# Attention values with v stationary in four column tiles, softmax sums from ScalarE's accumulator, own heads picked by DMA, and the end of the layer in later slots

## The reference, cut to what matters

```python
xn = _layernorm(x)
x = x + mamba(xn) + experts(xn)       # layer 0: conv, selective scan over N = 16 states; top-1 of 8 experts
xn = _layernorm(x)
x = x + attn(xn) + ffn(xn)            # layer 1

def attn(x, Wq, bq, Wk, bk, Wv, bv, Wo, bo):      # 16 heads of 8 channels, window of 64
    q, k, v = (_split_heads(x @ W + b) for W, b in ((Wq, bq), (Wk, bk), (Wv, bv)))
    scores = einsum('bhqd,bhkd->bhqk', q, k) / sqrt(8) + _sliding_window_mask(s, 64)
    probs = softmax(scores)
    return merge_heads(einsum('bhqk,bhkd->bhqd', probs, v)) @ Wo + bo

def ffn(x, w_gate, w_up, w_down):                 # int weights times 1/127, 384 hidden
    return (silu(x @ wg.T) * (x @ wu.T)) @ wd.T
```

## Time and profile before

| | before |
|---|---|
| time, median of 3 runs | 1190.73 us (1190.70 to 1194.21) |
| the profiled execution: its own time | 1193.12 us |
| its span in the trace | 1191.1 us, 13478 instructions |
| PE / DVE / ACT / POOL busy, share of the span | 78% / 71% / 51% / 35% |
| mean granted clock of PE | 0.923 of 2.4 GHz |

### The profile page before, as it was taken

One profiled execution on the slowest core, in us unless ns is written; L12 is line 12 of the kernel. 1 busy time (PEld: TensorE's weight loads), 2 busy tenths in 40 slices (PEclk: granted clock), 3 DMA queues, 4 the chain that ended last, 5 costly groups with the idle time before them and its releaser, 6 DMA issues.

```text
span 1191.1 us, 13478 instructions
## 1 busy us (share of the span) xinstructions
PE 923.4 (78%) x4474; PEld 585.3 (49%) x4474; DVE 849.0 (71%) x1301; ACT 613.0 (51%) x1410; POOL 411.1 (35%) x234
## 2 busy tenths in 40 slices
PE   3553888857887788778887788878787878788786
PEld 2412676734554455545454455545554545445555
DVE  7772543669779877888688868886978788767232
ACT  2142555635655655564566455655645564654542
POOL 2274222233622362237213722363226423532000
PEclk9566999987999899999999899989998999999998
DMA  8163878843322332233223321333233223430000
GB/s 277 40 216 125 235 234 294 239 110 86 81 65 75 90 82 73 66 79 89 73 70 90 89 73 54 90 92 87 54 80 87 76 66 83 99 80 1 10 1 9
DMA packets 79540, 116.65 MB, mean 98 GB/s; under 512 B 4848, under 2 KB 40048, under 8 KB 79344
## 3 DMA queue, kind: packets, MB, share of 16 engines
q1 hardware_dynamic: 73184, 108.99, 33.5%
q0 software_dynamic: 6288, 6.82, 2.5%
HBM read 103.73 MB, written 12.06 MB: 97 GB/s over the span
## 4 chain that ended last, share of the span: by engine, by line
PE 37%; DVE 19%; issue 17%; POOL 13%; ACT 10%; DMA 3%; SPq 0%; POOLq 0%; DVEq 0%; ACTq 0%
PE y_bank L1151 11%; DVE hst L705 7%; POOL hc L1066 7%; PE more L1240 7%; POOL xs_d L1034 3%; POOL x_res L1050 3%; ACT pexp L983 3%; PE work_l L1232 3%; DVE dBu L697 2%; ACT pT L988 2%; PE work_l L1226 2%; PE work L1232 2%; PE work L1170 2%; DMA hst<-in_hidden 1%; PE more L1248 1%
## 5 line engine op out<-in xcount | busy, mean ns | idle before, releaser
L1066 POOL TENSOR_TENSOR hc<-hst,bcr 128x1024 f32<-128x1024 f32 x116 | 280.2, 2415 | 607.8 <-DVE dBu L697 607.8
L1151 PE MATMUL y_bank<-hc,pk 128*128 128x512 f32 x512 | 275.0, 664 | 68.6 <-POOL hc L1066 59.7
L705 DVE TENSOR_TENSOR_SCAN hst<-dA,dBu 128x1024 f32<-128x1024 f32 x128 | 291.6, 2278 | 5.7 <-ACT dA L901 4.9
L1151 PEld LDWEIGHTS y_bank<-hc,pk 128*128 128x128 f32 x512 | 100.6, 208 | 183.9 <-POOL hc L1066 83.9
L901 ACT ACTIVATE dA<-dt,neg_a 128x511 f32<-128x511 f32 x256 | 171.4, 726 | 17.3 <-DVE hst L705 15.8
L697 DVE TENSOR_TENSOR dBu<-dtu,bcr 128x1024 f32<-128x1024 f32 x128 | 157.9, 1234 | 12.7
L1240 PE MATMUL more<-vw,pT 96*128 96x99 f32 x1024 | 131.0, 280 | 37.3 <-ACT pT L988 25.9
L1240 PEld LDWEIGHTS more<-vw,pT 96*128 96x128 f32 x1024 | 121.2, 194 | 69.3 <-issue 38.1
L988 ACT COPY pT<-work 96x512 f32<-96x512 f32 x64 | 37.2, 581 | 157.4 <-PE work L1232 157.4
L820 DVE TENSOR_REDUCE nmax<-work 128x4 f32<-128x384 f32 x64 | 35.4, 554 | 62.6 <-PE work L1226 62.6
L988 ACT COPY pT<-work_l 96x512 f32<-96x512 f32 x64 | 37.2, 581 | 63.9 <-PE work_l L1232 63.9
(11 more groups left out here) (296 smaller groups left out, 1422.0 us busy)
## 6 DMA issues: line engine op xcount, KB each, us to landing
bcr<-bc_d SPq DMA_DIRECT2D x128, 512.0 KB, 4.9
qbd<-in_wx SPq DMA_DIRECT2D x8, 578.0 KB, 3.9
attn<-in_wx SPq DMA_DIRECT2D x8, 578.0 KB, 4.3
pT<-in_wx SPq DMA_DIRECT2D x8, 578.0 KB, 5.7
kT<-in_wx SPq DMA_DIRECT2D x8, 578.0 KB, 5.3
vw<-in_wx SPq DMA_DIRECT2D x8, 578.0 KB, 5.0
xs_d<-rbuf POOLq DMA_DIRECT2D x1, 2560.0 KB, 9.7
hst<-in_hidden SPq DMA_DIRECT2D x8, 256.0 KB, 5.8
```

The source lines that it names most:

```text
L705: v.tensor_tensor_scan(hst[n % 2][:].rearrange("p h t -> p (h t)"), dA[n % 2][:].rearrange("p h t -> p (h t)"), dBu[:].rearrange("p h t -> ...
L1066: g_.tensor_tensor(hc[n % 2][:], hst[n % 2][:], bcr[n % RING][:, 1:2, :].to_broadcast([P, NH, L]), ALU.mult).then_inc(s_hc, 1)
L1151: last = t.matmul(y_bank[h][:], ident, hc[n % 2][:, h, :], start=False, stop=(n == N - 1))
```

## The change

1. `values` is turned round: v of one row group (96 keys x 32 channels) is stationary, pT (96 x 128) is moving, and the four r go to the partitions 32r to 32r+31 of the bank, that is, to four column tiles of PE. The result is already the transposed one, but each channel row holds all four heads' queries, and is not divided by the sum.
2. The sum comes from `accum_out` of the exponential on ACT (`den`). DVE takes one reciprocal of 128x64 in slot 27 (`rden`).
3. `averages` is now one ACT copy of 128x256 per two groups into `o_all`; the DVE work in it is gone.
4. In slot 0 (`rdT`) PE transposes the 128x64 reciprocals, ACT copies them, SP issues 16 DMAs that pick each head's own 8 rows of 2 KB out of `o_all` into `fth`, 4 DMAs that store the reciprocals in HBM, one that reads them back with each row repeated over 8 partitions, into `y_out`. In slot 5 (`avg`) POOL multiplies the two; in slot 6 ACT adds the bias (`attnT`).
5. `fin` moves from slot 3 to slot 7, `y_out` from slot 4 to slot 8.
6. After the third `ffn` tanh (slot 20), ACT loads the table set that holds both logarithm and exponential. The memset of `vw` to one (L679) is gone.

```diff
-LAYER1_AT = {... 6: ["v2", "v3"]}
-FINISH_AT = {2: ["attnT"], 3: ["fin"], 4: ["y_out"]}
-EDGE = [("attn", "y_end"), ("finish", "attnT"), ("pre", "xnT"), ("attn", "gated"), ("attn", "out")]
+LAYER1_AT = {... 6: ["v2", "v3"], 27: ["rden"]}
+FINISH_AT = {0: ["rdT"], 5: ["avg"], 6: ["attnT"], 7: ["fin"], 8: ["y_out"]}
+EDGE = [("attn", "y_end"), ("finish", "rdT"), ("pre", "xnT"), ("attn", "gated"), ("attn", "out")]
...
+                    if name == "rdT":                                   # SP
+                        done1(sp, b, f"gate{HC - 1}")
+                        done1(sp, b, f"o{G // 2 - 1}")
+                        for r in range(RG):
+                            for h in range(4):
+                                q = slice(32 * r + HD * h, 32 * r + HD * h + HD)
+                                sp.dma_start(o_own[q, :], o_all[q, h, :, :].rearrange("p g q -> p (g q)")).then_inc(s_own, 16)
+                        done1(sp, b, "rdT")
+                        for r in range(RG):
+                            rows = rd_d[b, r] if isinstance(b, int) else ...
+                            sp.dma_start(rows.rearrange("h g q -> g h q"), rdenT[r * G:(r + 1) * G, :, :]).then_inc(s_rdst, 16)
+                        sp.wait_ge(s_rdst, b * 64 + 64)
+                        before(sp, s_out, b * 16)
+                        sp.dma_start(rd_rows, rows.rearrange(...).unsqueeze(1).to_broadcast([RG * 4, HD, L])).then_inc(s_rdin, 16)
...
-                    v.memset(vw, 1.0).then_inc(s_clear, 1)
...
-                elif name == "averages":                                # DVE
-                    key = f"o{k // 2}"
-                    full1(dve, b, key)
...
-                    v.reciprocal(rden[:], o[:, :, :, 32]).then_inc(s_rden, 1)
...
-                        last = v.tensor_tensor(attn[:, k - 1:k + 1, :, j, :], o[q, :, :, HD * j:HD * j + HD],
-                                               rden[q, :, :].unsqueeze(3).to_broadcast([32, 2, RG, HD]), ALU.mult)
+                elif name == "rden":
+                    done1(dve, b, f"s{G - 1}")
...
+                    v.reciprocal(rden[:], den[:]).then_inc(s_rden, 1)
...
                         last = s.activation(pexp[k % 2][:, r, :], w1k(f"s{k}")[:, r * KW:(r + 1) * KW], ACT.Exp,
-                                            bias=nmax[:, k, r:r + 1])
+                                            bias=nmax[:, k, r:r + 1], accum_out=den[:, r, k:k + 1])
...
                     s.activation(fth[:], w1k(f"gate{k}")[:], ACT.Tanh).then_inc(s_fth, 1)
+                    if k == HC - 1:
+                        s.preload_act_table_set("natural_log_exp_and_others")
+                elif name == "averages":                                # ACT
+                    key = f"o{k // 2}"
+                    full1(act, b, key)
...
+                    s.copy(o_all[:, :, k - 1:k + 1, :].rearrange("p h g q -> p g h q"),
+                           w1k(key)[:, 0:2 * P].rearrange("p (g h q) -> p g h q", g=2, h=4)).then_inc(free1(key), 1)
+                elif name == "rdT":
+                    full1(act, b, name)
+                    before(act, s_rdst, b * 64)
+                    s.copy(rdenT[:].rearrange("p h q -> p (h q)"), w1k(name)[0:RG * G, 0:P]).then_inc(free1(name), 1)
                 elif name == "attnT":
-                    full1(act, b, name)
-                    s.activation(attnT[:], w1k(name)[:], ACT.Identity, bias=pc("bv")).then_inc(free1(name), 1)
+                    act.wait_ge(s_avg, b + 1)
+                    done1(act, b, f"up{HC - 1}")
+                    s.activation(attnT[:], fth[:], ACT.Identity, bias=pc("bv")).then_inc(s_attnT, 1)
...
+                    elif name == "avg":                                 # POOL
+                        pool.wait_ge(s_own, b * 256 + 256)
+                        pool.wait_ge(s_rdin, b * 16 + 16)
+                        g_.tensor_tensor(fth[:], fth[:], rd_rows, ALU.mult).then_inc(s_avg, 1)
...
                     for c in range(2):                                  # PE, values
                         for r in range(RG):
-                            a = (c * RG + r) * 33
-                            last = t.matmul(w1k(key)[:, a:a + VREP * 33].rearrange("p (n d) -> p n d", n=VREP),
-                                            pT[(k - 1 + c) % 4][:, r * P:(r + 1) * P],
-                                            vw[:, k - 1 + c, r, :].unsqueeze(1).to_broadcast([KW, VREP, 33]),
-                                            start=True, stop=True)
+                            last = t.matmul(w1k(key)[32 * r:32 * r + 32, c * P:(c + 1) * P], vw[:, k - 1 + c, r, :],
+                                            pT[(k - 1 + c) % 4][:, r * P:(r + 1) * P], start=True, stop=True)
...
-                elif name == "attnT":
-                    t.matmul(w1k(name)[:, 0:2], identb[:], identb[:, 0:2], start=True, stop=True)
-                    for g in range(G):
-                        last = t.transpose(w1k(name)[:, g * GQ:(g + 1) * GQ], attn[:, g, :, :, :]..., ident[0:GQ, 0:GQ])
+                elif name == "rdT":
+                    pe.wait_ge(s_rden, b + 1)
+                    t.transpose(w1k(name)[0:RG * G, 0:P], rden[:].rearrange("p r g -> p (r g)"), ident).then_inc(s_full1, 1)
```

57 lines of the change are left out of this document (30 added, 27 removed).

## The result

The changed kernel took 1178.99 us (median of 4 runs, 1174.6 to 1180.28), the kernel before 1192.47 on the same chip; the ratio is 0.9871, with a 95% interval of 0.9853 to 0.9889. The profiled execution took 1178.53 us, its span is 1176.7. The total is the forecast one. Its terms are not: several were wrong and cancelled, which is luck.

The account below looks back on a forecast made before the run. No engine is full, so hand-overs bound the turn. Six steady turns at -4.3 (-25.8), -1.2, -1.8 and +15.9 give -12.9 from 1193.1: 1180 profiled, 1178.5 us as median; range 1152 to 1206, the forecast's own 1167 to 1188.

Parts of the forecast that it names:

- Slots 21 to 27: End of a steady turn: table loads gone, less DVE work, clock kept up; DVE is last, gate 3.6 us earlier.
- Values: Values matmuls on PE, per two groups: 1.4 us instead of 2.00, as column tiles partly overlap; saving 0.6.
- The first rival: Column tiles on PE don't overlap, or mode changes cost the gain: values 1.8 us, total 1190.5; chance 0.2.
- Sums: Accumulator output on ACT's 64 exponentials a turn: lost overlap and a 65 ns read-out, 0.6 us per four.
- a: Extra ACT time per four exponentials for the accumulator output: taken as 0.6 us, between 0 and 1.44.
- Turns 7 and 8: Turn 7: -1.2 us, no table loads to save; turn 8: values and exponentials cancel, table load +1.3, `fin` +4.6.
- Slots 3 to 9 and 10 to 20, the term -0.7 - 0: Steady turn: values -1.8, exponentials +1.8, `averages` -0.7, together -0.7 us; slots 3 to 9: +0.3 and -0.3.
- DVE no longer waits for `y_out` but for this tanh. +0.3: Slots 3 to 9: transposes come 1.3 us earlier, but the tanh needs its 1.28 us table load; net +0.3.
- Price nothing: SP's queue at turn start: fourth `bcr` lands late, covered by a later wait of 5 us; uncovered, 2.5 us a turn.
- The scan sum after it runs in 2.0 instead of 3.78 us: Slots 3 to 9: `fin` fills PE's 5.02 us wait for POOL, so the next scan sum runs faster; part of -0.3.
- The table loads: ACT table loads at 1.28 us each by the profile row; with the skill page's drain, up to 2.8 us a turn more.
- The end, +10: Last values to last store: 19.5 us against 9.3 before, with 16 DMAs at 7.5 us.

Follow-up runs that it names:

- before_table: The kernel before plus only the load of the table with exponential and logarithm behind the third gate tanh; ratio 1.0031 to the kernel before.
- before_late_fin: The kernel before with only the attention-output transposes, output projection and `y_out` moved to slots 6 to 8; ratio 1.0091 to the kernel before.
- dve_back_small: The changed kernel plus a dummy reciprocal and one 128x64 product on DVE behind every second group; ratio 0.9888 to the kernel before.
- values_twice: The changed kernel with every group of 16 values matmuls issued twice into the same bank; ratio 0.9954 to the kernel before.
- rows_late: The changed kernel with POOL's four indirect loads of x_res in slot 18 instead of 10; 1155.52 us, ratio 0.9691 to the kernel before.

## Why the prediction was right, and where it was not

The forecast of 1178.5 met 1178.99 by luck: the direction and the gain in slots 21 to 27 were understood, but the terms differ by up to 11 us and cancel. They are in this table (us; measured from the table of turns):

| term | forecast | measured |
|---|---|---|
| turn 1, with the memset | -6.1 | -6.9 |
| turns 2 to 6 | 5 x -4.3 = -21.5 | -10.5 |
| turn 7 | -1.2 | -7.9 |
| turn 8 to the end of its last values | +5.9 | -2.4 |
| last values to the end | +10 | +13.5 |

**Slots 21 to 27, right.** -3.6 was forecast, with DVE as the last; -3.3 measured (31.5 to 28.2), and the new reciprocal is 0.55 instead of the 0.2 I put in. Its parts do not add up one by one: the table loads alone gave 1.0 (`before_table`) and the later projection alone gave 1.0 (`before_late_fin`, 30.5), but both by taking away the same wait of 0.96 us. DVE's products are worth 1.2 by `dve_back_small`. DVE gave up about 4.9 us of `averages` and 2.2 of waits for values in this stretch and got 3.1 of waits for scores back, so that what is left of the 3.3 is the interplay of both, not tested apart.

**Values, mis-sized.** "I take 1.4": 0.65, below the bound of 1.19 that I had made from the pace of small pairs. Column tiles beside each other go at 41 ns a pair; pairs on the whole array never showed that, so their pace was no bound for tiles. The first rival, no overlap, is excluded. The Trainium skill's "TensorE: Matmul & The Clock Gate" (Part 3, measured speedup) was on the right side: 2.38x for three tiles; here four tiles with 128 moving columns are 0.65 us against 1.8 at the pace of the transposes, 2.8x. (The ratio of that page of the Trainium skill on the 1.8 would have been an estimate of 0.76, which is 0.6 below my 1.4 and not the 0.2 that I wrote.) The Trainium skill's "TensorEngine Tiling (Array Packing)" (Key Properties) has a drain at each change of mode; PE's timeline shows none of any size, the scores' first matmul starts 0.58 us after the values:

```profile
1114.43 0.64 PE L1267 MATMUL more<-pT,vw 96*32 96x128 f32 x16 [0.76 <-ACT pT L998]
1115.01 0.34 PE L1252 MATMUL work_l<-bandb,identb 128*128 128x384 bf16 x1
```

**Sums, mis-sized.** a is 0.36 in place of 0.6. I had taken a short read-out; it is a long one that overlaps.

**Turns 7 and 8, the step that failed.** "8 times (0.6 - 0.6) = 0" and -1.2 for turn 7. With both sizes as measured, each two groups give -1.35 + 2 x 0.36 = -0.6: in turn 8 the period of two groups without ffn fell from 6.38 to between 5.36 and 5.99 us, and in turn 7 the middle third from 65.3 to 60.8. `values_twice` gives part of it back in both (3.2 and 2.4 us). Another 3.1 us of turn 8 are the last values themselves, 3.71 us at the lower clock before and 0.65 now. I had also counted one a per pair, where there are two groups in it.

**Slots 3 to 9 and 10 to 20, the term -0.7 - 0.** "DVE no longer waits for `y_out` but for this tanh. +0.3" came out (21.9 for 22.1). "Price nothing" for SP's queue came out only net: DVE waits 2.80 us for `bcr` in a steady start, and the cover that I named (a later tanh) is just as long. The middle lost 1.4 where I had forecast a gain of 1.0 (-0.7 and -0.3). The step that failed is that I counted savings on PE's path alone. They came (1.1 up to scan 8, 1.8 behind scan 10), but 4.3 us were lost between scans 8 and 10, where everything now meets POOL's four loads and the lengthened `dBu` (`rows_late` has all of it back). The later projection alone loses 2.0 at the same place (`before_late_fin`). "The scan sum after it runs in 2.0 instead of 3.78 us" was wrong, too; PE still waited for POOL there and fell to the lower clock. And two of five turns lose 2.3 us more by the clock.

**The table loads.** The row's 1.28 us holds again after; the drain that the Trainium skill's "ScalarE: Activation LUTs" (What ACT_TABLE_LOAD costs) gives is in no row here, as the tanh begins 1.29 us after its load (761.64 to 762.93 above).

**The end, +10.** 22.8 us against 19.5 forecast. The 16 issues took 11.0 instead of 7.5, which is as much as the difference.

So the errors were +11.0 in the steady turns and +3.5 at the end, against -6.7 in turn 7, -8.3 in turn 8 and -0.8 in turn 1: their sum is -1.3 us (and turn 1 began 0.3 earlier).
